# Two place values of a step packed into one integer that TensorE takes apart in registers (graph network, attention and convolution stages, one core)

## The reference

```python
# layer 2: attention
h = x @ W
e = leaky_relu(s_src[src] + s_tgt[tgt], 0.2)
m = segment_max(e, tgt); e_exp = exp(e - m[tgt])
h_prime = elu(segment_sum(h[src] * (e_exp / segment_sum(e_exp, tgt)[tgt]), tgt))
# layer 3: two convolutions, the second on relu of the first
norm = dinv[src] * dinv[dst]
out = segment_sum((x @ Wk)[src] * norm, dst) + b
```

## Time and profile before

| | us |
|---|---|
| median of 3 runs | 14837.96 |
| lowest, highest run | 14833.63, 14841.61 |
| profiled execution, its own time | 14940.95 |
| its span, first to last instruction | 14939.1 |

### The profile page before, as it was taken

One profiled execution on the slowest core, in us unless ns is written; L12 is line 12 of the kernel. 1 busy time (PEld: TensorE's weight loads), 2 busy tenths in 40 slices (PEclk: granted clock), 3 DMA queues, 4 the chain that ended last, 5 costly groups with the idle time before them and its releaser, 6 DMA issues.

```text
span 14939.1 us, 182194 instructions
## 1 busy us (share of the span) xinstructions
PE 8307.1 (56%) x46670; PEld 7582.8 (51%) x46671; DVE 6695.0 (45%) x13205; ACT 2723.1 (18%) x6542; POOL 8996.6 (60%) x8046
## 2 busy tenths in 40 slices
PE   5777787765555555578845555563333334333334
PEld 5777777754445444477745554463333333333333
DVE  6444444434444444489945565564222223222223
ACT  0111111101111111266623333340000000000000
POOL 3888888873556655500037777754666664666664
PEclk7666666666666667799967677775555555555555
DMA  4333333332333333332212222221111111111111
GB/s 91 18 18 18 18 18 18 18 51 68 97 96 98 98 99 96 99 100 98 94 47 66 66 68 67 67 65 27 23 23 23 23 23 26 23 23 23 23 23 23
DMA packets 851085, 769.36 MB, mean 51 GB/s; under 512 B 652784, under 2 KB 660804, under 8 KB 848965
## 3 DMA queue, kind: packets, MB, share of 16 engines
q0 software_dynamic: 446272, 333.87, 16.1%
q1 hardware_dynamic: 249485, 294.83, 5.9%
q10 hardware_dynamic: 155282, 140.11, 3.1%
HBM read 569.49 MB, written 197.82 MB: 51 GB/s over the span
## 4 chain that ended last, share of the span: by engine, by line
issue 23%; another core or an unknown queue 19%; PE 18%; POOL 15%; DVE 10%; DMA 8%; DVEq 5%; ACT 1%; ACTq 0%; POOLq 0%; SPq 0%
POOL lane_tab L679 9%; DMA lane_tab<-rows,idx 7%; POOL tab L703 6%; PE ps L1127 3%; PE ps L1153 3%; PE ps L1128 3%; DVEq L469 2%; DVE acc_w L1797 2%; DVEq L458 1%; DVE buf_d L469 1%; PE ps L1192 1%; PE ps L1178 1%; PE ps L1168 1%; PE ps L1113 1%
## 5 line engine op out<-in xcount | busy, mean ns | idle before, releaser
L703 POOL DMA_INDIRECT tab<-gcn_tab,idx x3136 | 2983.1, 951 | 1807.3 <-issue 1232.9
L679 POOL DMA_INDIRECT lane_tab<-rows,idx x1664 | 2598.3, 1561 | 616.8 <-issue 616.8
L703 POOL DMA_INDIRECT tab<-att_tab,idx x1568 | 1739.2, 1109 | 1923.1 <-DVEq L1684 1311.1
L1168 PE MATMUL ps<-tab,buf_d 128*128 x3328 | 795.2, 387 | 2162.6 <-issue 2121.8
L1168 PEld LDWEIGHTS ps<-tab,buf_d 128*128 128x128 f32 x3328 | 781.0, 320 | 2249.3 <-issue 2249.3
L1797 DVE TENSOR_TENSOR acc_w<-acc_w,ps 128x512 f32 x416 | 286.1, 688 | 3395.9 <-remote 3108.7
L693 POOL DMA_INDIRECT buf_b<-src_tab,idx x832 | 825.6, 992 | 749.4 <-ACT idx L813 296.4
L693 POOL DMA_INDIRECT acc_w<-src_tab,idx x832 | 838.0, 1007 | 598.0 <-ACT idx L813 335.1
L1065 PE MATMUL ps<-ident,srcg 128*128 128x128 f32 x3328 | 721.9, 405 | 659.6 <-DVE srcg L1430 655.1
L1168 PE MATMUL ps<-tab,buf_a 128*128 x3328 | 762.8, 424 | 531.7 <-issue 403.3
L1168 PEld LDWEIGHTS ps<-tab,buf_a 128*128 128x128 f32 x3328 | 725.9, 330 | 650.5 <-issue 650.1
(11 more groups left out here) (283 smaller groups left out, 16942.2 us busy)
## 6 DMA issues: line engine op xcount, KB each, us to landing
y_stash<-buf_c SPq DMA_DIRECT2D x208, 512.0 KB
tab<-y_stash SPq DMA_DIRECT2D x208, 512.0 KB, 3.3
aux<-dst_rows ACTq DMA_DIRECT2D x104, 512.0 KB
buf_b<-dst_rows ACTq DMA_DIRECT2D x104, 512.0 KB
tab<-gcn_tab,idx POOLq DMA_INDIRECT x3136
aux<-in_edge_attr_dram ACTq DMA_DIRECT2D x848, 32.0 KB
aux<-in_edge_attr_dram SPq DMA_DIRECT2D x848, 32.0 KB
lane_tab<-rows,idx POOLq DMA_INDIRECT x1664
```

What stands on the lines that cost most here:

```text
L679: pool.indirect_dma_start(lane_tab[k][:, :], bass.IndirectOffsetOnAxis(ap=idx[:, b, u:u + 1], axis=0), rows[:, b, u, 0:D1], None, compute_ ...
L703: pool.indirect_dma_start(to[k][:, u, :], None, table[:, :], bass.IndirectOffsetOnAxis(ap=idx[:, k % RING, u:u + 1], axis=0)).then_inc(row ...
L1168: last = pe.matmul(ps_flat[:, bass.ds(rel[u] + q * 512, D)], g_hot[q][:, u, :], g_ring[:, bass.ds(at[u], D)], start=False, stop=True, skip ...
```

## The change

The table's at column keeps, for the convolutions, rel in its lowest three bits and at above them; for attention the rel column holds the packed value, and the at column stays for ScalarE. TensorE loads 9 values of a group in the convolutions (8 packed and `needed`, from value 17 g + 8) and 8 in attention (from 17 g). Then `unpack` takes each apart: an AND with 7 and a multiply by the stride for rel, a right shift by 3 for at. The waits, the matmuls, the gathers and their order stay as they are. In VectorE's tables one instruction is added for attention, and none for the convolutions.

```diff
--- before.py
+++ after.py
@@ -62,6 +62,7 @@
 D1 = D + 1
 D2 = D + 2
 GP = 2 * G + 1
+PACK = G.bit_length() - 1
 PLACES_AT = LONG * G * D2
 ZEROS = 195
 MASK = 2.0 ** 40
@@ -433,14 +434,22 @@
 
         PLACES_WHY = "the table's entries are made from clamped step places"
 
-        def load_steps(g, places=g_places, stride=P // 2, n=D, ring=LONG):
+        def unpack(v, stride, n, ring):
+
+            return ([nc.s_assert_within((a & (G - 1)) * stride, 0, (G - 1) * stride, skip_runtime_bounds_check_because=PLACES_WHY) for a in v],
+                    [nc.s_assert_within(a >> PACK, 0, (ring * G - 1) * n, skip_runtime_bounds_check_because=PLACES_WHY) for a in v])
+
+        def load_conv_steps(g):
             _, v = nc.values_load_multi_w_load_instructions(
-                places[:, bass.ds(g * GP, GP)], engines=(mybir.EngineType.PE,), min_val=0, max_val=(ring * G - 1) * n,
+                g_places[:, bass.ds(g * GP + G, G + 1)], engines=(mybir.EngineType.PE,), min_val=0, max_val=(LONG * G * D << PACK) - 1,
                 skip_runtime_bounds_check_because=PLACES_WHY)
-            tops = [(G - 1) * stride] * G + [(ring * G - 1) * n] * G
-            v = [nc.s_assert_within(a, 0, t, skip_runtime_bounds_check_because=PLACES_WHY) for a, t in zip(v, tops)] + [
-                nc.s_assert_within(v[2 * G], RING + 1, RING * (TT + 1))]
-            return v[0:G], v[G:2 * G], v[2 * G]
+            return *unpack(v[0:G], D, D, LONG), nc.s_assert_within(v[G], RING + 1, RING * (TT + 1))
+
+        def load_l2_steps(g):
+            _, v = nc.values_load_multi_w_load_instructions(
+                l2_places[:, bass.ds(g * GP, G)], engines=(mybir.EngineType.PE,), min_val=0, max_val=(L2_RING * G * D2 << PACK) - 1,
+                skip_runtime_bounds_check_because=PLACES_WHY)
+            return unpack(v, P, D2, L2_RING)
 
         def load_rows(g):
             _, v = nc.values_load_multi_w_load_instructions(
@@ -1162,7 +1171,7 @@
                         pe.matmul(ps[:, q, :].rearrange("p (k f) -> p k f", f=P), zero_b[:, :],
                                   bc(ident_b[:, :].unsqueeze(1), [P, 4, P]), start=True, stop=False, skip_group_check=True)
                         pe.wait_ge(left_ready, g + 1)
-                        rel, at, needed = load_steps(g)
+                        rel, at, needed = load_conv_steps(g)
                         pe.wait_ge(landed, needed)
                         for u in range(G):
                             last = pe.matmul(ps_flat[:, bass.ds(rel[u] + q * 512, D)], g_hot[q][:, u, :], g_ring[:, bass.ds(at[u], D)],
@@ -1250,7 +1259,7 @@
                 for c in range(2):
                     pe.matmul(ps[:, bank + c, :].rearrange("p (k f) -> p k f", f=P)[:, :, 0:D1], zero_b[:, :],
                               bc(ident_b[:, 0:D1].unsqueeze(1), [P, 4, D1]), start=True, stop=False, skip_group_check=True)
-                rel, at, _ = load_steps(g, l2_places, P, D2, L2_RING)
+                rel, at = load_l2_steps(g)
                 pe.wait_ge(s.l2_hots, g + 2)
                 for u in range(G):
                     last = pe.matmul(ps_flat[:, bass.ds(rel[u] + bank * 512, D1)], l2_hot[q % 2][:, u, :], l2_ring[:, bass.ds(at[u], D1)],
@@ -1666,7 +1675,9 @@
             link(dve.tensor_scalar(turn_row, turn_row, 18, None, ALU.arith_shift_right))
             link(dve.scalar_tensor_tensor(turn_row, turn_row, -float(L2_RING * G), row_s[:, 0:S], ALU.mult, ALU.add))
             link(dve.tensor_scalar(l2_steps[:, :, G:2 * G], turn_row.rearrange("p (a u) -> p a u", u=G), float(D2), None, ALU.mult))
-            link(dve.tensor_copy(l2_steps[:, :, 0:G], rel_grp))
+            link(dve.tensor_scalar(l2_steps[:, :, 0:G], rel_grp, 1.0 / P, None, ALU.mult))
+            link(dve.scalar_tensor_tensor(l2_steps[:, :, 0:G], turn_row.rearrange("p (a u) -> p a u", u=G), float(D2 << PACK),
+                                          l2_steps[:, :, 0:G], ALU.mult, ALU.add))
             link(dve.tensor_tensor(new_win[:, 1:S], win_all[:, 1:S], win_all[:, 0:S - 1], ALU.not_equal))
             link(dve.memset(new_win[:, 0:1], 1.0))
             link(dve.tensor_scalar(new_win[:, 0:S], new_win[:, 0:S], -2.0 * MASK, None, ALU.mult))
@@ -1759,8 +1770,8 @@
             link(dve.scalar_tensor_tensor(sums_d, sums_d, 0.0, x_n[:, :, :], ALU.max, ALU.add))
             needed_tiles(g_steps)
             link(dve.tensor_scalar(row_s[:, 0:S], row_s[:, 0:S], LONG * G - 1, None, ALU.bitwise_and))
-            link(dve.tensor_scalar(g_steps[:, :, G:2 * G], row_grp, float(D), None, ALU.mult))
-            link(dve.tensor_scalar(g_steps[:, :, 0:G], rel_grp, float(D) / P, None, ALU.mult))
+            link(dve.tensor_scalar(g_steps[:, :, G:2 * G], rel_grp, 1.0 / P, None, ALU.mult))
+            link(dve.scalar_tensor_tensor(g_steps[:, :, G:2 * G], row_grp, float(D << PACK), g_steps[:, :, G:2 * G], ALU.mult, ALU.add))
             dve.wait_ge(s.elu_out, 1)
             link(dve.scalar_tensor_tensor(sums_d, rest_d, -1.0, sums_d, ALU.add, ALU.add))
             norm(sums_d, 3, scratch=rest_d)
```

## The result

The changed kernel takes 15,009.41 us in the median of 4 runs (14,973.02 to 15,104.67), the kernel before 14,839.78 us in 4 (14,833.63 to 14,901.12): a ratio of 1.0088, 95% interval 1.0055 to 1.0122. By this ratio it is slower by some 130 us (the two medians lie 170 us apart), four times the bound of 0.2%. The forecast was 14,822 within 14,640 to 14,890, with 0.17 for slower.

What follows compares the result with a forecast made beforehand. POOL was taken to pace the steady convolutions and attention, PE's sequencer the convolutions' ends. Ends −14, attention's end −2, one more DVE instruction +1: −15 us from 14,838, taken as 14,822; range 14,640 to 14,890.

Steps and rivals of the forecast that it cites:

- The load's mechanism and its prices: TensorE's table load: off a multiple of 16 bytes 2.14 us for nine values, 1.90 for eight; on it 0.85 and 0.59.
- The ends' gain from the load alone: Convolution ends, after POOL's last gathers: shorter loads save 6.2 us in each of six turns, 37 us with unpacking fully fused.
- the price of the unpacking: TensorE's sequencer: up to 16 more instructions a group, up to 85 ns each, 2.3 to 5.4 us a turn, middle 3.9.
- the slower rival: Convolutions' q1 and q2: new instructions outweigh loads from 0.19 us more a matmul; at 0.26, 204 us, 15,027; chance 0.17.
- The forecast's −14 us: Convolution ends: six turns' load savings less the unpacking's cost, 5 to 23 us won, middle 14.
- In the steady stretches: nothing: Steady stretches: no gain or loss, since TensorE reaches q1's end 31 us before it is seen.
- about cancel: Steady turn: q3's matmuls left after the release, 1 to 2 us more, against shorter loads of q1 and q2.
- More than two thirds: Convolutions: TensorE's matmuls idle "by issue" for over two thirds of their time, pointing at its sequencer.
- POOL paces the steady stretch: Steady stretch of a convolution: 32 gathers take 40.0 us, plus one 5.9 us stall, a turn of 45.8 us.
- The stall didn't go with shorter loads: Faster rival, steady convolutions: q0 ending 0.97 us earlier removes POOL's stall, 572 us, 14,251; milder form 14,708; chance 0.29.
- The change did reach the load: Rival: new load starts off the multiple of 16 in all groups, 6 us saved in all; within the likeliest case's 0.54.

Runs made afterwards that it cites:

- after_again: The changed kernel unchanged, rerun where the kernel before took 13,358 us beside it; ratio 1.0011.
- aligned_packed: The changed kernel with its table rows padded to 20 values; ratio 1.0078 to the kernel before.
- short_load: The kernel before with the convolutions' load cut from 17 to 9 values, no unpacking, each matmul's window place a constant; ratio 0.9962.
- one_op: The change in the convolutions alone, packed so that the AND goes: two sequencer instructions a matmul; ratio 1.0020 to the kernel before.
- more_ops: The kernel before with an AND and a shift more for each convolution matmul, all 17 values still loaded; ratio 1.0144.
- before_again: The kernel before unchanged, rerun for its profile where it took 13,358 us; ratio 0.9997.
- aligned: The kernel before with table rows padded from 17 to 20 values, nothing packed; ratio 0.9958.
- conv_packed: The changed kernel without its attention part, so the change in the convolutions alone; ratio 1.0107 to the kernel before.
- att_packed: The change in attention alone, convolutions as in the kernel before; ratio 0.9995.

## Why the prediction was wrong

**What held.** The load's mechanism and its prices: the fourth group on a multiple of 16 bytes, 2.17 us off it for nine values (forecast 2.14), 0.85 on it (0.85; the least of line 443 in after_again), 1.93 for eight (1.90). That the steady stretch doesn't see the load's length, as long as TensorE isn't what POOL waits for (aligned_packed shows the other case). The ends' gain from the load alone: forecast 6 turns × 6.2 = 37 us, measured 37 in short_load.

**The step that failed first: the price of the unpacking, "85 ns" a slot at most.** A group's address instructions at full speed, behind the last gather, first in the kernel before and then after (first and last start of each):

```profile
L1168 PEldq FUSED_REGOPS  x8: 64/64/69, 12464.7 to 12465.7; - x8
```

```profile
L1177 PEldq FUSED_REGOPS  x16: 60/66/76, 14859.6 to 14862.4; - x16
L1177 PEldq ALU_OP  x8: 32/32/36, 14859.7 to 14862.3; - x8
```

From the first matmul's instruction to the eighth's it is 1.0 us, so 0.14 for a matmul; with three (by the ALU operations, one a matmul) it is 2.6 us, some 0.37. So two instructions more cost 0.23 us for each matmul, 0.115 each in the mean, though they last 32 and 66 ns: the duration isn't the slot. That is 7.4 us a turn, over the 6.2 that the loads win, and over the 0.19 us for a matmul at which the slower rival was to decide. Nor is 0.115 a price for any instruction: in one_op a single one more, of another form, costs 0.22. The 85 ns came from dividing a group's time outside its load by a guessed 20 instructions, and from taking it that this time was all the sequencer's. The ends show it. Groups of the changed kernel behind the last gather, to be held against the earlier trace rows:

```profile
14865.65 3.67 PE L1177 MATMUL ps<-tab,buf_d 128*128 x16 [1.62 <-issue]
...
14871.44 3.67 PE L1177 MATMUL ps<-tab,buf_d 128*128 x16 [1.69 <-issue]
```

They are 5.79 us apart, as before: the 1.9 us that the load gave, the unpacking has taken. From the last gather to the end it is 160.8 us after and 151.9 before, since TensorE is also further behind when POOL stops (14.2 groups left for 12.7). The forecast's −14 us was +9 at the very end, and +2 between the convolutions.

**The step that cost most: "In the steady stretches: nothing", "about cancel".** It saw the 16 instructions at up to 1.4 us each in the slow stretch, and then held the sum at full speed against them. But in a slow stretch an instruction's length at full speed says little: in the kernel before q3's load of 17 values took 1.38 us in it at 11331.8, for 4.04 at full speed, and in the changed kernel fused and ALU operations take up to 1.41 us each for their 0.07 and 0.03. So the short load wins little there and the 16 instructions can lose much. TensorE now comes to the limit of POOL's head start, and POOL waits for it twice in five groups. 2,315.4 − 2,238.7 = 77 us a convolution, 1.6 us for four groups. The slower rival had this place and nearly this size (2.1 us a turn, 204 us in all, for a chance of 0.17); the runs more_ops, one_op and short_load show that the added instructions are the cause. What one costs in a slow stretch they don't show. Counted from the traces of a convolution's gathers, matmuls that stand over 0.7 us behind the one before in their group are 4.2 us apart in the kernel before, 2.3 in one_op and 2.9 in the changed kernel: from two instructions to three it is 0.6 us more, but with one the two records of a matmul come singly (2.8 us apart in the earlier trace rows) where with two or three they come as a pair. Why, stays open, and so it would be wrong to multiply a slot's price by a count.

In the prediction's rows two readings were loose as well. "More than two thirds" idle holds for q2 and q3 alone (2,162.6 us idle beside 795.2 busy); on q0 and q1 it is 531.7 beside 762.8. And that POOL paces the steady stretch is half of it: a convolution has 208 groups of steps for 196 of tiles, and at every stall TensorE stood where POOL stood, while in before_again it is 11 groups ahead at a convolution's last gather. That is why there were three turns left for the ends at all. (The turn's work at full speed is 20.2 us, not 20.3; nothing hangs on it.)

**The other rivals.** The stall didn't go with shorter loads: the gathers of short_load and aligned last 2,238 us as ever. But its condition, a q0 that ends 0.97 us earlier, was met in neither: after the release it ends at 7.7 us in the median in the kernel before and in aligned, at 7.4 in short_load. So this rival didn't come true here and stands untested beyond 0.4 us. The change did reach the load. The rule of the Trainium skill (Runtime: NRT & Kernel Launch, Instruction fetch mechanics) of some 200 ns a register fits the loads off the multiple of 16 bytes (0.24), and not those on it (0.07 to 0.09). The other rule of the Trainium skill (Perfetto Trace Analysis, Identifying the Most-Contended Engine) would have said 0: POOL has the highest occupancy and its work didn't change. In after_again that is what came, 1.0011; in the slow condition, with 1.0088, POOL waits for TensorE's sequencer, whose instructions count as busy nowhere.

**Open.** What makes the slow stretches. They stand beside POOL's gathers, and in the kernel before, during them, POOL's sequencer was itself blocked (line 701 let go at 11324.8 and then at 11354.3); but the same kernels ran without any in before_again and its neighbours, on a chip of the same number (5) as conv_packed, att_packed, more_ops and short_load, which had them. And slow register instructions aren't the condition itself but one of its signs: of the 1,641 us between the two profiles of the kernel before, 705 lie ahead of attention, 254 in it and 682 behind, and in layer 1 the address instructions take 46 ns in both. Why an increment of TensorE's is seen so late in them wasn't tried either.

## What to carry to other kernels

Look at a sequencer's instructions by their distance, not by their durations: take it from one matmul's address instruction to the next in a stretch where nothing else holds them, and take it again from the edited kernel, since one more cost 0.22 us here and two more 0.23. Then look for stretches where they are slow, and count them there. Before a table is packed to shorten its load, look at how its rows lie: padding 17 values to 20 cut the load from 4.04 to 1.36 us, gained 0.4% (0.9935 to 0.9980), added nothing and cost nothing where nothing was slow (0.9994), which makes it the version to keep here; packing them cut it to 2.17 and lost 0.9%. If packing is needed, choose a form that the compiler fuses (shift, multiply, subtract) over an AND: 0.2% slower (0.9994 to 1.0045) instead of 1.1% for the convolutions.

## What was unexpected of the hardware

A TENSOR_LOAD of 17 values takes 1.36 us if it begins on a multiple of 16 bytes and 4.04 if not. The three address instructions of a matmul last 32 to 76 ns and start 0.10 to 0.14 us apart; two of another form take as long together, 0.36 us. The same kernel before took 14,840 to 14,897 us (medians) in some sets of runs and 13,300 to 13,358 in others; in the former profiles TensorE's address instructions in the convolutions take up to 1.4 us for stretches of some 10 to 26 us beside GpSimd's gathers, in the latter none takes over 0.09. So some 10% of this kernel's time hangs on a condition that isn't in the program, and so does what an edit costs: the change is slower by 0.9% in the one and equal within 0.3% in the other.
